# Attention outputs of head pairs summed into feature rows beside their denominators, output transposes left out, and biased keys copied from PSUM by ScalarE

## What is computed

```python
scores = jnp.einsum('bhqd,bhkd->bhqk', Q, K) / jnp.sqrt(jnp.float32(D_K))
scores = jnp.where(mask_bhqk, scores, -jnp.inf)
attn = jax.nn.softmax(scores, axis=-1)
out = jnp.einsum('bhqk,bhkd->bhqd', attn, V)
return _merge_heads(out) @ wo
```

## Time and profile before

| | |
|---|---|
| median of 3 runs | 1161.72 us (1161.29 to 1163.68) |
| the profiled execution | 1159.94 us, of which 1157.7 us from its first to its last instruction (the span) |
| PE busy | 1106.9 us, 96% of the span |
| DVE, ACT, POOL busy | 841.3 us, 618.6 us, 258.8 us |
| DMA | 45.11 MB in all, most of it in the first 58 us |

### The profile page before, as it was taken

One profiled execution on the slowest core, in us unless ns is written; L12 is line 12 of the kernel. 1 busy time (PEld: TensorE's weight loads), 2 busy tenths in 40 slices (PEclk: granted clock), 3 DMA queues, 4 the chain that ended last, 5 costly groups with the idle time before them and its releaser, 6 DMA issues. The chain is left out here.

```text
span 1157.7 us, 36414 instructions
## 1 busy us (share of the span) xinstructions
PE 1106.9 (96%) x13908; PEld 921.1 (80%) x13908; DVE 841.3 (73%) x3468; ACT 618.6 (53%) x1584; POOL 258.8 (22%) x383
## 2 busy tenths in 40 slices
PE   6999999999999999999999999999999999999886
PEld 5878778888778788878888887888888878787665
DVE  4466987957878687697687777786778685987841
ACT  3644455455555556545556565655556455545453
POOL 0322412203121230222304032320321223121100
PEclk9999999999999999999999999999999999999997
DMA  9600010200111001010010202001010100110000
GB/s 339 246 11 2 2 48 11 84 20 2 28 40 28 39 16 52 2 41 26 16 52 2 66 2 66 2 16 52 16 52 2 52 2 2 52 47 7 2 6 10
DMA packets 21224, 45.11 MB, mean 39 GB/s; under 512 B 2496, under 2 KB 14912, under 8 KB 18112
## 3 DMA queue, kind: packets, MB, share of 16 engines
q1 hardware_dynamic: 19952, 41.36, 10.1%
q10 hardware_dynamic: 1104, 1.44, 0.4%
HBM read 40.70 MB, written 2.10 MB: 37 GB/s over the span
## 5 line engine op out<-in xcount | busy, mean ns | idle before, releaser
L663 POOL TENSOR_TENSOR root<-var_eps,halves 128x1 f32<-128x1 f32 x128 | 76.9, 602 | 609.9 <-DVE var_eps L1171 588.1
L971 ACT ACTIVATE exps_t<-bank 128x512 f32<-128x512 f32 x256 | 135.7, 605 | 34.3 <-PE bank L795 33.8
L1111 DVE CUSTOM_DVE_ANT_0 bank<-bank,bias 128x128 f32<-128x128 f32 x512 | 130.1, 324 | 18.8 <-PE bank L763 18.8
L721 PE MATMUL bank<-x_t,weights_A 128*128 128x128 f32 x1024 | 139.3, 284 | 2.7 <-ACT x_t L931 2.1
L721 PEld LDWEIGHTS bank<-x_t,weights_A 128*128 128x128 f32 x1024 | 127.3, 197 | 12.1 <-ACT x_t L931 4.5
L721 PE MATMUL bank<-x_t,weights_F 128*128 128x128 f32 x1024 | 127.9, 281 | 2.8 <-ACT x_t L931 1.7
L721 PEld LDWEIGHTS bank<-x_t,weights_F 128*128 128x128 f32 x1024 | 121.6, 195 | 9.1 <-ACT x_t L931 3.1
L808 PE MATMUL bank<-exps_t,v_one 128*32 128x128 f32 x3072 | 114.5, 277 | 8.2 <-DVE exps_t L1083 6.1
L714 PE MATMUL bank<-weights_F,exps_t 128*128 128x256 f32 x512 | 121.1, 383 | 0.2 <-DVE neg_max L1111 0.2
L763 PE MATMUL bank<-k_eo,q_t 32*128 32x256 f32 x1536 | 107.7, 396 | 2.6 <-issue 1.7
L1111 DVE DVE_READ_ACCUMULATOR2_ANT neg_max<- 128x1 f32 x768 | 106.5, 139 | 0.1
(11 more groups left out here) (112 smaller groups left out, 1964.8 us busy)
## 6 DMA issues: line engine op xcount, KB each, us to landing
weight<-in_fside SPq DMA_DIRECT2D x16, 1024.0 KB, 4.9
weights_A<-in_weights_A SPq DMA_DIRECT2D x4, 1028.0 KB, 15.3
weights_F<-in_weights_F SPq DMA_DIRECT2D x2, 2054.0 KB, 17.9
drop_raw<-in_drop SPq DMA_DIRECT2D x16, 256.0 KB, 5.3
x_hat<-in_x SPq DMA_DIRECT2D x16, 128.0 KB, 2.5
out<-x_sum SPq DMA_DIRECT2D x16, 128.0 KB, 1.7
ctx_t<-in_ctx_t SPq DMA_DIRECT2D x13, 128.0 KB, 3.0
rows_A<-in_rows_A SPq DMA_DIRECT2D x3, 512.0 KB, 15.4
```

The costliest lines, as they stand in the source:

```text
L663: nc.gpsimd.tensor_tensor(root[x][:], var_eps[x][:], halves[:, e:e + 1], ALU.pow).then_inc(done["root"], 1)
L721: mm = nc.tensor.matmul(dst[:, 128 * f:128 * f + 128], w[:, c, 128 * f:128 * f + 128], tokens_t[:, c, :], start=(c == 0), stop=(c == KC - 1))
L971: nc.scalar.activation(dst, score_bank(x, "ST", s, j)[:], ACT.Exp, scale=DH ** -0.5).then_inc(done["exp"], 1)
L1111: ins = nc.vector.tensor_tensor_reduce(out=heads[:, n, :], in0=heads[:, n, :], in1=mask_bias(x, s), scale=-1.0, scalar=2.0 ** 126, op0=ALU ...
```

## The change

**Outputs.** The values of two heads of neighbouring parity are kept as 48 columns, 16 of one, 16 zeros, 16 of the other (`v_pairs`). A window of 32 columns is either (values, zeros) or (zeros, values), so two matmuls that accumulate in the same 32 rows put two heads' features one below the other. Four such pairs fill the 128 rows of a chunk, which are then the rows that the output product wants. The same with ones for values (`ones_pair`) gives, in two more chunks of the same bank, each feature row's denominator. A `PV` beat now covers eight heads in 16 matmuls; there are two of them a stage. `o_raw`, `oT`, `nT` and `o_t` are gone. VectorE inverts 128x256 denominators and multiplies 128x256 outputs from PSUM straight into `q_t`.

**Keys with a bias.** ScalarE writes them in four instructions of 128x128, with scale and bias, where VectorE had two of 128x256.

**First loads.** The inputs and contexts of the first six batches are issued alternately from SyncE and ScalarE, in the order in which TensorE takes them; the key masks come behind SyncE's three inputs.

**Orders.** All tables are new.

```diff
-        yield from (("PV", s, j) for j in range(GROUPS))
+        yield from (("PV", s, half) for half in range(HALVES))
         if ATTN[s]["feeds"]:
             yield "V", ATTN[s]["feeds"]
-        yield from (("oT", s), ("nT", s), ("O", s))
+        yield "O", s
...
 TENSOR = """
-12345112112332124001001124551111001122210200010202203000120100001023032323103000230330303010011011201124101000001221
+31245223323311240010024001222153052200020010000011021103311300001003320120123341040000011101130130314220222200012003
...
+        v_pairs = per_set("v_pairs", [128, H // 2, 3, DH])
+        ones_pair = sb("ones_pair", [128, 3, DH])
...
+        o_t, recip = q_t, x_t
...
-                load_x(sp, 0)
+                for x in FIRST[::2]:
+                    load_x(sp, x)
                 load_keys(sp)
-                for x in range(1, SETS):
-                    load_x(sp, x)
...
+                def of_pair(values, odd):
+                    return values[:, odd:odd + 2, :].rearrange("p a d -> p (a d)")
...
-                    for n in range(GH):
-                        mm = nc.tensor.matmul(bank((x, "PV", s, 0))[32 * n:32 * n + 32, 128 * j:128 * j + 128], v_one[x][:, VE * head(j, n):VE * head(j, n) + 2 * DH],
-                                              exps_t[EXP_AT[x, s]][:, GH * j + n, :], start=True, stop=True)
+                    for chunk in (half, KC + half):
+                        for odd in range(2):
+                            for at, (j, c) in enumerate((j, c) for j in groups for c in range(KC)):
+                                values = v_pairs[x][:, GROUPS * c + j] if chunk < KC else ones_pair
+                                mm = nc.tensor.matmul(bank((x, "PV", s, 0))[32 * at:32 * at + 32, 128 * chunk:128 * chunk + 128],
+                                                      of_pair(values, odd), exps_t[EXP_AT[x, s]][:, GH * j + 2 * c + odd, :],
+                                                      start=(odd == 0), stop=(odd == 1), skip_group_check=True)
                     mm.then_inc(done["PV"], 1)
...
+                        if s in biased:
+                            act.wait_ge(keys_biased, 2 * biased.index(s) + 2)
+                            for odd in range(2):
+                                for c in range(KC):
+                                    ins = nc.scalar.activation(k_eo[x][:, c, odd, :], src[:, c, :], ACT.Identity,
+                                                               bias=k_bias[s][:, odd, c:c + 1], scale=parity[:, odd:odd + 1])
...
-                    dve.wait_ge(done["oT"], nth(x, "oT", s))
-                    heads = bank((x, "oT", s))[:].rearrange("p (h e) -> p h e", h=H)
-                    nc.vector.reciprocal(recip[x][:].unsqueeze(2), heads[:, :, DH:DH + 1]).then_inc(recip_made, 1)
+                    dve.wait_ge(done["PV"], nth(x, "PV", s, HALVES - 1))
+                    chunks = bank((x, "PV", s, 0))[:].rearrange("p (c q) -> p c q", c=2 * KC)
+                    nc.vector.reciprocal(recip[x][:], chunks[:, KC:, :]).then_inc(recip_made, 1)
                     dve.wait_ge(recip_made, nth(x, "o_norm", s))
-                    nc.vector.tensor_tensor(o_norm[x].rearrange("p (h d) -> p h d", h=H), heads[:, :, 0:DH],
-                                            recip[x][:].unsqueeze(2).broadcast_to([128, H, DH]), ALU.mult
-                                            ).then_inc(done["o_norm"], 1)
+                    nc.vector.tensor_tensor(o_t[x][:], chunks[:, 0:KC, :], recip[x][:], ALU.mult).then_inc(done["o_norm"], 1)
```

More of the change, by code:

```diff
@@ L173, in scalar_lane @@
             continue
-        if ATTN[s]["kv"] == "self" and not ATTN[s]["b"]:
+        if ATTN[s]["kv"] == "self":
             yield "k_eo", s
@@ L181, in scalar_lane @@
         feeds = ATTN[s]["feeds"]
-        if feeds and not ATTN[feeds]["b"]:
+        if feeds:
             yield "k_eo", feeds
-        yield "o_raw", s
         if feeds and not ATTN[feeds]["b"]:
             yield "v", feeds
-        yield "o_t", s
         yield from (("square", n) for n in LNS_AFTER[s] if n in SQUARED)
@@ L302 @@
         NTH[_beat] = _seen[_beat[1]] = _seen.get(_beat[1], 0) + 1
-TAKEN_BY = {"fold": "folded", "xT": "x_t", "K": "k_eo", "Q": "q_t", "V": "v", "mT": "m_t", "oT": "o_norm", "nT": "o_t", "O": "sum",
-            "Y": "sum", "H": "h_t"}
+TAKEN_BY = {"fold": "folded", "xT": "x_t", "K": "k_eo", "Q": "q_t", "V": "v", "mT": "m_t", "O": "sum", "Y": "sum",
+            "H": "h_t"}
 SCORES = ("S", "ST")
@@ L330 @@
 EXP_AT, EXP_BEFORE = shared_places(EXP_PLACES, [b for b in SCALAR_ORDER if b[1] in ("exp", "h_t") and b[3] == 0])
-OUT_AT, OUT_BEFORE = shared_places(OUT_PLACES, [b for b in SCALAR_ORDER if b[1] == "o_raw"])
+FIRST = [beat[0] for beat in TENSOR_ORDER if beat[1:] == ("xT", "A0") and beat[0] < SETS]
 WEIGHT_TURNS = [beat[0] for beat in SYNC_ORDER if beat[1] == "load_weight"]
@@ L396, in program @@
         x_t = per_set("x_t", [128, KC, N])
-        o_norm = [t[:].rearrange("p c q -> p (c q)") for t in x_t]
         ctx_t = per_set("ctx_t", [128, KC, N])
@@ L413, in program @@
         exps_t = [sb(f"exps_t{b}", [128, H, N]) for b in range(EXP_BUFFERS)]
-        o_raw = [sb(f"o_raw{b}", [128, GROUPS, N]) for b in range(OUT_BUFFERS)]
-        recip = per_set("recip", [128, H])
-        o_t = q_t
+        o_t, recip = q_t, x_t
         bn = per_set("bn", [128, 6])
@@ L452, in program @@
         stored = sems("stored")
-        done = {k: sem(f"done_{k}") for k in ("xT", "K", "Q", "S", "V", "mT", "ST", "shift", "PV", "oT", "nT", "O",
+        done = {k: sem(f"done_{k}") for k in ("xT", "K", "Q", "S", "V", "mT", "ST", "shift", "PV", "O",
                                               "H", "Y", "fold")}
-        done |= {k: sem(f"done_{k}") for k in ("x_t", "square", "v_copy", "k_copy", "q_t", "m_t", "exp", "o_raw", "o_t", "h_t")}
+        done |= {k: sem(f"done_{k}") for k in ("x_t", "square", "v_copy", "k_copy", "q_t", "m_t", "exp", "h_t")}
         done |= {k: sem(f"done_{k}") for k in ("bias", "pairs", "folded", "k_eo", "v", "times", "lower", "max", "high_low", "keep", "o_norm", "sum",
@@ L481, in keys_made @@
         def keys_made(s):
-            return done["k_eo" if ATTN[s]["b"] else "k_copy"]
+            return done["k_copy"]
         def values_made(s):
@@ L510, in taken @@
             elif kind == "PV":
-                taker = ("o_raw", s)
+                taker = ("o_norm", s)
             elif kind == "V":
@@ L525, in slots @@
             return slice(GH * j, GH * j + GH)
-        def heads_of(values):
-            return values[:, 0:H * VE].rearrange("p (h e) -> p h e", h=H)
         def hidden(x, s):
@@ L900, in free_exponentials @@
                     else:
-                        engine.wait_ge(done["PV"], nth(y, "PV", t, GROUPS - 1))
+                        engine.wait_ge(done["PV"], nth(y, "PV", t, HALVES - 1))
             def free_keys(engine, x, s):
```

184 lines of the change are left out of this document (74 added, 110 removed).

## The result

The changed kernel takes **1273.84 us** (median of 3 runs, 1272.91 to 1274.9) where the kernel before took 1161.72: 1.0961 times as long (95% interval 1.0936 to 1.0986). The forecast was 1175 us with a range up to 1196. The sign was right, the size was not: 112 us came, 13 were forecast.

The account below looks back on a forecast made before the run. The prediction took PE's own work to bound the middle and chains of dependent steps the end. PE's work +17.8, hand-off +6 and end -9 sum to +14.8 on 1159.94: 1175 us, range 1156 to 1196.

Parts of the forecast that it names:

- the hand-off from PV to O with DVE's queue: Between output matmuls and output product: a 2.2 us wait, mostly covered by other batches' PE work, DVE's queue included; +6 us.
- the inversion binds DVE: Rival, slower still: inversion of 2.3 us or more brings DVE to 85%; 1189 us, above 1200 at 4.0 us; chance 0.14.
- my 905 to 935: Sign of being right: DVE busy for 905 to 935 us.
- my slope: VectorE's 128x256 inversion, priced at 5.8 ns an element from 128x1 and 128x16 inversions: 1.64 us.
- PE's own work: On PE: outputs +83.3 us, dropped transposes -62.4, shape changes about -3; together +17.8 us.
- pause for accumulating pairs: Rival: strips drain between a pair's two matmuls; +54 us at most, 1229, or 1190 at a third; chance 0.05.
- 275 ns a transpose: Skill's price for PE's dropped transposes: the six would save 158 us, ending near 1085; left 1 in 100.
- the 10 to 20: Sign of being right: PE's busy time rises by 10 to 20 us.
- the end, -9: From batch 14's last `ST` to the end: last two batches side by side, 35 us instead of 52.6; -9 us booked.
- biased keys on ACT: Keys moved to ScalarE: 1.14 us a group, 73 us in all, ACT at half load; booked 0.
- two hops fewer: Faster rival: dropped beats and waits on copies free the order; 1153 us with all the middle's idle; chance 0.21.
- it cancels: Rival: the new order brings what PE's added work costs, 15 us; 1160 to 1164 us; chance 0.12.

Follow-up runs that it names:

- e1: Changed kernel with VectorE's 128x256 inversion replaced by a copy of the same tile: 1184.32 us, ratio 1.0208 to the kernel before.
- e5: Changed kernel with a copy in place of the inversion and a 128x256 inversion into a spare tile behind the product: 1276.68 us, ratio 1.0991.
- e6: Changed kernel with the first 128 of the 256 denominators inverted and the other 128 copied: 1222.41 us, ratio 1.0529.
- e12: Changed kernel with a copy in place of the inversion and biased keys written without bias by two 128x256 instructions: 1182.54 us, ratio 1.0184.
- e9: Changed kernel, same instructions, with other order and place tables from a search replaying trace durations: 1123.62 us, ratio 0.9676.
- e11: Kernel before, same instructions, with order and place tables of its own from the same search: 1121.36 us, ratio 0.9654.
- e13: Changed kernel, inversion kept, with biased keys written without their bias by two 128x256 instructions: 1272.33 us, ratio 1.0956.
- e8: Kernel before with the biased keys moved from VectorE to ScalarE, at the place where VectorE wrote them in time: 1213.93 us, ratio 1.0451.
- e10: Changed kernel with the tables of e9 and a copy in place of the inversion: 1124.88 us, ratio 0.9681.
- e4: Kernel before with an added 128x256 inversion into a spare tile directly behind each output product on VectorE: 1268.54 us, ratio 1.0921.
- e2: Kernel before with an added 128x256 inversion into a spare tile ahead of each 128x16 one: 1298.16 us, ratio 1.1211.

## Why the prediction was wrong

**The step that failed is the hand-off from PV to O with DVE's queue, +6 us.** I had written that PE work of other batches covers it and that uncovered it would show 133 us. It was two thirds uncovered: in the order that was run, a copy in place of the inversion gives back 89.5 us (e1). Two things were wrong with my count. I counted only PE's work between each `PV` and its own `O` (17.9 us missing), and so priced a hand-off. e5 shows that most of it is the queue: behind the product, where no `O` of its batch waits for it, an inversion still costs 92 us. And I took DVE's 79% of the time as room. My reading of why it was none: both orders are fixed, so a longer beat moves all later DVE beats, which move PE's, which move DVE's next ones; idle time elsewhere in a queue takes that up only where it lies behind the long beat and before the next meeting of the two engines. The runs give the pass-through in numbers. Of one us more on DVE in the changed kernel 0.52 to 0.94 came through (e6; 0.70 over the whole, e1) and 0.55 behind the product (e5); in the kernel before it was 0.82 ahead of the product and 0.63 behind it, and 0.84 on PE.

**The rival "the inversion binds DVE" came nearest in mechanism, but not by its own condition.** It asked for 2.3 us or more; the inversion takes 1.75, 0.11 more than my slope gave, 11 us over 96 of them. DVE is busy for 930.8 us, inside my 905 to 935. It didn't become the bound by its sum. The Trainium skill's "VectorE: DVE Perf Modes", sections "First, the fixed hardware budget" and "Specifications", gave an estimate of 2.13 us; the trace has 1.75.

**Right: PE's own work.** The output groups hold 6144 records, at 0.44 us for sixteen (684.47 to 684.93 to 685.37 in the timeline of outputs, 0.22 for eight). There was no pause for accumulating pairs. e12, without the inversion's and the keys' length, is 21.3 us above the kernel before, beside the +17.8 for PE's work; the two can't be split further, since e1's middle has 38.7 us of PE idle in 984 (before: 20.4) and the end gains. By the 275 ns a transpose that I had set aside (the Trainium skill, "TensorE: Matmul & The Clock Gate", Part 4) e12 would lie 96 us lower, which no run shows. (My sum for that rule was off: 96 us below 1174.7 is 1079, not 1085.) PE's busy time rose by 32.9 us, though, outside the 10 to 20 that I had named as a sign of being right: I had left out what waits add, the clock above all. In e9, at a clock of 0.995, it is 13.7 us above e11.

**Right: the end, -9.** Batch 14's last `ST` starts at 1235.53; this is the window from there to the end:

```profile
1235.53:1271.20 35.67, 25.60 (x334) 22.23 (x333) 15.57 (x50) 13.49 (x33) 2.62 (x4) 0.95 0.04 12
```

35.7 us where I walked 35 and where the earlier trace rows has 52.6. Of these 16.9 us, 5.6 are work that now stands earlier, by my prices; 11 are waits, and I had booked 9.

**A size: biased keys on ACT.** 1.14 us a group was read from an instruction with a bias alone. With bias and scale by partition four take 1.53 us (635.42 in ACT's timeline), 97.3 us and not 73. ACT's total came to 625.4 us, not about 600. In the changed order the longer part of that cost nothing that the runs can tell (e12, e13). That it was to be free because "ACT is at half load" is the wrong reason: in e8 the same move costs 52 us, with ACT at 58% (53% before).

**The rivals "two hops fewer" and "it cancels"** did not come in the order that was run, but the second one came in e9 and e11. Each in an order of its own, the designs are 2.3 us apart (their ratios' intervals, 0.9659 to 0.9693 and 0.9637 to 0.9672, overlap): PE is busy 13.7 us more in e9 (1093.5 against 1079.8), and idle 14.7 less (27.7 against 42.4). So PE's extra work is paid back by less waiting. That the hand-overs that are gone do it is my reading; how near each order is to its design's best was not tested.

**What stays open.** Which durations the changed order was laid out for was not tested; that a copy in place of the inversion doesn't make it fast (e1 is still 60 us above e10) says that the inversion's length isn't all that it lacks. How much is due to each table, TensorE's or VectorE's, was not tried either.

## What to carry to other kernels

In a kernel whose engines run fixed orders, price an added instruction by its queue, not by its engine's load or by the one hand-off that it stands in. In these runs, in orders that were left as they were, half to nine tenths of an added length came through on engines that were 53 to 73% busy, about as on the one that was full. The list of waits names the beat that came last, not the one that pushed it back: moving the length behind the hand-off (e4, e5) is what told the two apart. And before judging a design, lay its order out again with measured durations: 150 us lay in the changed kernel's order, 40 in the order of the kernel before, and 2 between the designs. Taking length out of a fixed order repays it only where that order was short of it: 128 us off DVE gave 89 in one order and nothing in another.

## What the runs showed of the hardware

- An inversion on VectorE costs by the element, at any width in these runs: 128x1 164 ns, 128x16 251 ns (194 directly behind another inversion, e2), 128x128 952 ns (e6), 128x256 1751 ns; a copy of 128x256 is 418 ns. From 16 elements on the slope is 6.2 ns an element ((1751 - 251) / 240); a copy takes 1.6 ns an element in all.
- ScalarE's instruction of 128x128 from PSUM, back to back, has a slot of 0.38 us with scale and bias by partition (four in 1.53 us) and 0.285 with another function and a bias alone (four in 1.14).
- 32-row accumulating pairs of matmuls cost TensorE what the same number of single ones cost, 0.22 us for eight records.
- A wait could cost TensorE twice. Behind 4.44 us of idle the granted clock stood at 0.50, and 32 records of `ST` took 2.09 us where they take 1.17 at full clock (changed kernel, 271.82 and 686.36 us).
